# Decoder block on one core: smaller operation pieces, new orders on four engines, and two feed-forward products in each other's PSUM bank

## What is computed

```python
x = _layernorm(x + attn(x))        # silu(x Wq), silu(x Wk), rotary, decayed causal linear attention,
                                   # chunks of 128 with a carried state, 16 heads of 16,
                                   # o * sigmoid(x Wg1 Wg2), rms-norm per head, times weight, @ Wo
x = _layernorm(x + experts(x))     # 4 experts picked by token id: (silu(x Wg.T) * (x Wu.T)) @ Wd, all three = ctx
x = _layernorm(x + ffn(x))         # conv over two steps along the batch axis, silu; q, k, v, g products; rotary;
                                   # routed masked attention over 4 steps; norm per head; silu(g) * o @ Wout
```

## Time and profile before

| | us |
|---|---|
| median of 3 runs | 273.94 (273.74 to 274.32) |
| the profiled execution, its own time | 274.79 |
| its span, first to last instruction | 272.4 |
| PE busy | 188.1 (69%) |
| DVE busy | 158.8 (58%) |
| POOL busy | 104.3 (38%) |
| ACT busy | 88.2 (32%) |
| mean granted clock of PE | 0.876 of full |

### The profile page before, as it was taken

How to read it: one execution, slowest core, us unless ns; L and a number is a source line. 1 busy time by engine, 2 the same in 40 slices (tenths; PEclk the granted TensorE clock), 3 DMA queues, 4 the chain that set the end, 5 groups by cost and what they waited for, 6 DMA issues and landing times.

```text
span 272.4 us, 3513 instructions
## 1 busy us (share of the span) xinstructions
PE 188.1 (69%) x1066; PEld 122.6 (45%) x1066; DVE 158.8 (58%) x437; ACT 88.2 (32%) x227; POOL 104.3 (38%) x190
## 2 busy tenths in 40 slices
PE   3689999996939795957985068978427057872442
PEld 2277755563516362716874036747214034431221
DVE  1127767979794979581672072062397353599831
ACT  0065444452612452323422023543301014651121
POOL 9740107343550423120443540210433822764533
PEclk9999999999977999799999559999955759998557
DMA  7993051000000000040244700101100200110011
GB/s 199 316 348 128 2 215 56 2 1 0 23 0 0 20 2 19 2 150 6 93 166 167 250 22 0 40 3 37 39 19 0 58 20 0 39 40 0 0 39 39
DMA packets 16273, 17.44 MB, mean 64 GB/s; under 512 B 2928, under 2 KB 13696, under 8 KB 16256
## 3 DMA queue, kind: packets, MB, share of 16 engines
q1 hardware_dynamic: 13328, 14.57, 16.1%
q0 software_dynamic: 768, 2.10, 2.4%
q10 hardware_dynamic: 2160, 0.56, 1.1%
HBM read 7.79 MB, written 5.77 MB: 50 GB/s over the span
## 4 chain that ended last, share of the span: by engine, by line
PE 38%; DVE 30%; issue 10%; DMA 8%; POOL 6%; ACT 4%; SPq 1%; ACTq 1%; POOLq 0%; DVEq 0%
PE bank L1190 16%; PE bank L1248 7%; PE bank L1395 4%; PE bank L1410 4%; DMA w_qk<-in_L_attn_Wk 3%; PE bank L1185 2%; DVE rcos L835 2%; DMA yg<-ys_d,pos 2%; DVE newton L826 2%; DVE newton L825 2%; DMA xs<-xs_d 2%; POOL rstd L361 2%; DVE stats L887 2%; PE bank L1292 2%; POOL yg L407 1%
## 5 line engine op out<-in xcount | busy, mean ns | idle before, releaser
L1248 PE MATMUL bank<-qx,kT 128*128 128x512 f32 x64 | 33.3, 646 | 13.3 <-DVE probs L857 12.0
L1190 PE MATMUL bank<-f_w,oT 128*128 128x512 f32 (+4 forms) x80 | 31.8, 549 | 5.8 <-ACT oT L643 5.8
L358 POOL TENSOR_SCALAR rstd<-agg 128x1 f32<-128x1 f32 x24 | 5.7, 239 | 70.7 <-DVE agg L889 70.3
L572 ACT ACTIVATE qx<-bank,con 32x256 f32<-32x256 f32 x64 | 26.3, 458 | 15.9 <-PE bank L1185 15.3
L1190 PEld LDWEIGHTS bank<-f_w,oT 128*128 128x128 f32 x80 | 16.2, 213 | 19.3 <-issue 8.9
L1248 PEld LDWEIGHTS bank<-qx,kT 128*128 128x128 f32 x64 | 11.8, 197 | 28.7 <-issue 26.4
L344 POOL TENSOR_TENSOR rsin<-qk,rope_tab 128x256 f32<-128x256 f32 x16 | 12.5, 802 | 31.8 <-ACT qk L555 31.7
L857 DVE TENSOR_TENSOR probs<-bank,con 128x512 f32<-128x512 f32 x32 | 21.5, 686 | 5.4 <-PE bank L1248 5.0
L958 DVE TENSOR_TENSOR rsin<-rcos,bank 128x512 f32<-128x512 f32 (+1 forms) x8 | 5.0, 620 | 27.3 <-ACT rcos L620 27.3
L1410 PE MATMUL bank<-slot_w,rsin 128*128 128x256 f32 x56 | 14.9, 409 | 8.2 <-DVE rsin L958 8.2
L1190 PE MATMUL bank<-w_qk,xT 128*128 128x512 f32 x32 | 17.2, 665 | 2.2 <-DMA w_qk<-in_L_attn_Wk 2.2
(11 more groups left out here) (149 smaller groups left out, 410.6 us busy)
## 6 DMA issues: line engine op xcount, KB each, us to landing
slot_w<-ctxT SPq DMA_DIRECT2D x14, 256.0 KB, 2.3
xs_d<-xs SPq DMA_DIRECT2D x2, 896.0 KB, 8.3
xs<-xs_d SPq DMA_DIRECT2D x2, 896.0 KB, 5.3
ys_d<-qkr SPq DMA_DIRECT2D x6, 256.0 KB, 2.2
x_sb<-in_x SPq DMA_DIRECT2D x4, 256.0 KB, 7.6
ctx_sb<-in_ctx SPq DMA_DIRECT2D x1, 1024.0 KB, 11.2
out<-x_sb SPq DMA_DIRECT2D x8, 128.0 KB, 1.7
con<-shape_constants SPq DMA_DIRECT2D x1, 402.5 KB, 3.1
```

What stands on the lines that cost most here:

```text
L358: eng.tensor_scalar(rstd[:, n, i:i + 1], agg[:, n, i, 1:2], LN_EPS, None, ALU.add)\
L572: eng.activation(qx[rr, i % 2, :, 2 * r + par, :], two(bank[2][rr, 0:2 * P]), ACT.Copy, scale=con[rr, C_PARITY + par:C_PARITY + par + 1]). ...
L1190: last = eng.matmul(dst, lhsT[:, k, :], w[:, k, :], start=(k == 0), stop=(k == KT - 1))
L1248: eng.matmul(bank[3 + g % 2][:, :], kT[:, i % 2, g // 2, :], qx[:, i % 2, g // 2, 4 * (g % 2):4 * (g % 2) + 4, :].rearrange("p h n -> p (h ...
```

## The change

The change does five things.

1. It cuts operations into smaller pieces: `proj_qkv` into `proj_qk`, `proj_v` and (with the first loop) `proj_gate`; `transpose_qk` into `turn_q` and `turn_k`; `attend(i)` into `attend(i, g)` for g = 0 to 3; `norm_o` into `square_o` and `root_o`; the turning of the experts' weights, the router weights and the centring of the value weights into calls of their own. Each piece keeps its instructions and takes the waits that it needs.
2. It drops `attention_round` from use. PE, DVE, ACT and POOL each get a new flat list of all calls from the first to the last. Nothing is computed that was not computed before, and the counts of operations are the same but for four more ACT_TABLE_LOAD on ACT (eight in place of four), since silu and sigmoid now alternate at the start.
3. `load_slots` issues four transfers, one per item, in place of one.
4. The q-v-k product of `project_step` goes to bank 4, and `project_out` to bank 6, with the waits that the banks' earlier users need.
5. The wait for cleared buffers at the head of ACT's list moves to the first `copy_v` and `expand_q`.

```diff
             def load_slots(c):
                 eng.wait_ge(S_(f"scattered{c}"), 16 * L)
-                if c:
-                    eng.wait_ge(S_("xsT_made"), len(ITEMS))
-                eng.dma_start(xs[:, :, :], xs_d[c][:, :].rearrange("(s q) d -> q s d", q=P)).then_inc(S_("xs_in"), 16)
+                for m, (s0, s1) in enumerate(ITEMS):
+                    if c:
+                        eng.wait_ge(S_("xsT_made"), m + 1)
+                    eng.dma_start(xs[:, s0:s1, :], xs_d[c][s0 * P:s1 * P, :].rearrange("(s q) d -> q s d", q=P))\
+                       .then_inc(S_(f"xs_in{c}{m}"), 16)
...
-            def attend(i):
+            def attend(i, g):
...
-                for g in range(4):
-                    eng.wait_ge(S_("probs"), 4 * i + g + 1)
+                eng.wait_ge(S_("probs"), 4 * i + g + 1)
...
-            def norm_o(i):
+            def square_o(i):
...
+                if i:
+                    eng.wait_ge(S_("o_rstd"), i)
                 eng.tensor_reduce(oms[:, :], heads(osq[:, i % 2, :]), AX.X, ALU.add).then_inc(S_("o_ms"), 1)
+
+            def root_o(i):
                 eng.wait_ge(S_("o_ms"), i + 1)
...
                 else:
                     eng.wait_ge(S_("wv_centred"), 2)
-                    eng.wait_ge(S_("ln0_sum"), TILES)
-                project(bank[6][:, :], uT[:, j % 2, :, :], f_w1[:, :, :]).then_inc(S_("f1_made"), 1)
+                    eng.wait_ge(S_("probs"), 4 * TILES)
+                project(bank[4][:, :], uT[:, j % 2, :, :], f_w1[:, :, :]).then_inc(S_("f1_made"), 1)
...
+                else:
+                    eng.wait_ge(S_("ln0_sum"), TILES)
                 for l in range(l0, l1):
-                    project(bank[4][:, (l - l0) * D:(l - l0 + 1) * D], fT[:, l - l0, :, :], f_out[:, :, :])\
+                    project(bank[6][:, (l - l0) * D:(l - l0 + 1) * D], fT[:, l - l0, :, :], f_out[:, :, :])\
...
             route_weights(0)
             weigh_values(0)
+            gate_values(0)
+            gather(4)
+            gather(5)
+            gather(6)
+            gather(7)
+            ln_rstd(1, 4)
+            scale_values(0)
...
-            for i in range(TILES - 1):
-                attention_round(i)
...
+            proj_qk(4)
+            turn_expert(2)
+            turn_expert(3)
+            turn_q(1)
+            turn_k(1)
+            scores(0, 0)
```

More of the change, by code:

```diff
@@ L1332, in attention_round @@
             def attention_round(i):
[L1333 removed]
+                turn_q(i)
+                turn_k(i)
                 if i == 0:
[L1335 removed]
+                    for n in range(E):
+                        turn_expert(n)
                     rank_tokens()
                 if 0 <= i - 1:
[L1338 removed]
+                    for g in range(4):
+                        attend(i - 1, g)
                 if i < L:
@@ L1479, in _ @@
-            transpose_qk(7)
-            attend(6)
-            for g in range(4):
-                scores(7, g)
+            turn_wg1()
+            transpose_x(0)
+            transpose_x(1)
+            make_wg()
+            proj_v(0)
+            transpose_x(2)
+            proj_gate(0)
+            proj_qk(0)
+            transpose_x(3)
+            transpose_x(4)
+            proj_gate(1)
+            proj_gate(2)
+            proj_gate(3)
+            transpose_x(5)
+            transpose_x(6)
@@ new lines, in _ @@
+            scores(2, 0)
+            scores(2, 1)
+            attend(1, 0)
+            attend(1, 1)
+            attend(1, 2)
+            attend(1, 3)
+            turn_k(3)
+            transpose_on(0)
+            proj_qk(5)
+            scores(2, 2)
+            scores(2, 3)
+            make_state(3)
+            scores(3, 0)
+            scores(3, 1)
+            project_o(0)
+            turn_back(1)
+            attend(2, 0)
+            attend(2, 1)
+            attend(2, 2)
+            scores(3, 2)
@@ new lines, in _ @@
+            proj_v(4)
+            attend(2, 3)
+            scores(3, 3)
+            turn_q(4)
+            turn_back(2)
+            proj_qk(6)
+            proj_v(5)
+            attend(3, 0)
+            attend(3, 1)
+            attend(3, 2)
+            attend(3, 3)
+            turn_q(5)
+            turn_k(4)
+            transpose_on(1)
+            proj_qk(7)
+            turn_k(5)
+            scores(4, 0)
+            scores(4, 1)
+            project_o(1)
+            scores(4, 2)
@@ new lines, in _ @@
+            attend(4, 0)
+            turn_back(3)
+            scores(4, 3)
+            attend(4, 1)
+            scores(5, 0)
+            turn_k(6)
+            turn_q(6)
+            attend(4, 2)
+            transpose_on(2)
+            attend(4, 3)
+            scores(5, 1)
+            proj_v(6)
+            turn_k(7)
+            scores(5, 2)
+            scores(5, 3)
+            project_o(2)
+            turn_q(7)
+            attend(5, 0)
+            turn_back(4)
+            attend(5, 1)
```

736 lines of the change are left out of this document (496 added, 240 removed).

## The result

| | us |
|---|---|
| median before (4 runs beside it) | 274.13 (273.74 to 275.01) |
| median after (4 runs) | 226.31 (224.66 to 228.00) |
| ratio, with its 95% interval | 0.825 (0.818 to 0.832) |
| the profiled execution after, its own time / its span | 224.66 / 222.6 |

In a later batch the same kernel had a median of 223.99 (223.48 to 229.74, 6 runs), so it spreads more than before did. Four of these six took 223.5 to 224.0 us and two 228.2 and 229.7.

A forecast was written before the change was run, and what follows sets the result against it. No engine was full; in attention DVE and PE were near full, DVE tighter, and later waits left half 1 nearly alone. Terms 116 + 27.5 + 8 + 26.5 + 9.5 + 53.5 gave 241.0 us of span, hence 242.5 us; range 231 to 258.

The forecast's parts named there:

- End of the masks: Start through attention's last mask: first mask at 41.3 us, masks ending at 116, 6.6 us sooner.
- DVE then has 64.7 us of work left: Masks' stretch: DVE's busy work from the first mask on, with 10.2 us of waits added.
- the narrower: Masks' stretch before: DVE (70.2 of 88.6 us busy) and PE (73.6) near full, DVE taken as the tighter limit.
- End of masks to first gather: Last mask to first gather of half 0: 27.5 us, 0.7 sooner; PE's item queue unchanged.
- Gather to h2: First gather of half 0 to first h2 transposition: unchanged at 8.0 us, PE's first half 1 item filling the gap.
- h2 to gathers of half 1: First h2 transposition to half 1's first gather: 26.5 us, 27.2 sooner, set by PE's work before the last down product.
- Gather to step 4: Half 1's first gather to tile 4's feed-forward product: 9.5 us, 0.5 later; bounds 9 to 13.
- Step 4 to the end: Last stretch: 53.5 us, 2.6 later; half 0's leftover DVE work mostly fits into waits, but the end chain stays unfilled.
- Banks: Exchange of banks for the feed-forward products: costs nothing; if not, half a microsecond.
- Table loads: Start, ACT: eight loads instead of four add 5.1 us, helping put the first mask at 41.3 us, not 34.
- better case: DVE waits only 5 us in attention and the last stretch takes 50: 234 us, chance 0.10.
- the rivals: No attention gain (249.5 us, 0.17); half 0 leftover unhidden (254.2, 0.13); better (234, 0.10); PE clock falls (0.04); no effect (0.01).

The follow-up runs named there:

- a1: Changed kernel's functions (four slot loads, exchanged banks, attend in four pieces) with every engine in the order of the kernel before: 270.31 us.
- b1: Changed kernel with one more score product on PE in each of tiles 1 to 7: 229.11 us.
- b2: Changed kernel with nine more mask products on DVE into an unread tile: executions of 224.93, 226.60, 230.61 and 231.08 us.
- a2: Changed kernel with the new lists up to the last masks and the old order behind them: 254.27 us.
- a3: Changed kernel with the old lists up to the last masks and the new order behind them: 243.47 us.
- c2: Changed kernel with one load of all slots of a half (896 KB) in place of four: 230.32 us.
- a4: As a1, but POOL's four half 1 gathers stand behind weigh_values(1), and DVE's residual2(4) and residual2(5) before head_var(1): 268.92 us.
- e1: Changed kernel with twelve more DVE reductions into an unread tile, four each ahead of the steps of groups 2, 3 and 4: 227.55 us.
- c1: Changed kernel with the feed-forward's q-v-k and output products back in banks 6 and 4, without the added waits: 225.96 us.
- c3: Changed kernel with ACT's eight sigmoids in one run and PE's gate products 5 to 7 earlier, for fewer table loads: 227.32 us.
- d0: Changed kernel unaltered, measured again in a later batch: 223.99 us.
- d2: d1 plus the edit of c3 (sigmoids in one run, gate products 5 to 7 earlier): 228.58 us.
- b3: Changed kernel with POOL turning the keys of steps back 2 and 3 inside attention instead of before the first mask: 230.03 us.
- c4: Changed kernel with tile 7's way to the slots moved earlier on PE and ACT, and half 1's slot loads before half 0's last store: 230.92 us.
- d1: Changed kernel with DVE's mark_experts moved from behind copy_xT(2) to behind copy_kT(0): 230.12 us.
- d3: d1 with SP's load of half 1's slots ahead of the fetch of slot 6's weights: 231.20 us.

## Why the forecast was wrong

**End of the masks** (116, measured 106.0): the step that failed is "DVE then has 64.7 us of work left", with a wait of 10.2 us laid on top. It had 55.8. The waits (10.6) came out as forecast by chance, since they are now DVE's waits for PE, and the first mask came 1.7 us sooner than forecast. Of the 8.9 us, some 5 are the root chains: 15.5 us for 60 steps in a1 (L912, L914 to L916) against 10.4 after. Cosines, squares and scalings, slowed in the same way, add 1.1 (by their means in the two kernels). The other 2.6 are work put in the wrong place: a third cosine, one scaling of h and one difference of the router weights no longer stand in the stretch (0.9, 0.5, 0.4), and the square and the sum of tile 6 do not come into it (0.8). I took durations of DVE from a trace in which POOL stood beside them, as if they were fixed, and moved POOL's work away without pricing it.

The second fault weighs more: I called DVE "the narrower" and made the sum for DVE alone. PE's sum is 73.6 us less three q-k products (24 matmuls stand there in a1 and 12 after, 6.0 us) and one v product (1.0) = 66.6 us, which from 39.6 on ends at 106.2. The longer of the two sums sets the end, and that is PE's, as b1 and b2 show; b2 also shows that 4.7 us of work put back on DVE cost 2.0, so right durations alone would not have mended the forecast much. That 66.6, worked out with the result at hand, comes so near the measured 66.26 is in part luck: it leaves out the first item of the experts, whose turning and upward products came into the stretch (2.6 us), and what PE's score and output products gained as the clock went from 0.94 to 1.00 (1.6 us, 32.5 to 31.5 and 5.8 to 5.2).

**End of masks to first gather** (27.5, measured 23.7): what failed is "PE is busy 21.5 of it and the queue of items is the same". PE is busy for 18.50 us: the first item's 20 matmuls (2.6 us) were done before the last mask. a2, with the new attention and the old lists behind it, has 22.2 us here, and a3, with the old attention and the new lists behind, 26.9, so the gain is the new attention's. On the old order the four loads shorten the stretch by 2.4 us (25.8 in a1), but in the new order by less than 1 (24.5 in c2).

**Gather to h2** (8.0, measured 8.5): right. The first item's product fills the gap as said, though PE stood idle 5.96 us ahead of it, and the split of the load is what keeps the 8.5 (10.3 in c2).

**h2 to gathers of half 1** (26.5, measured 24.8): the mechanism was right, PE's work in front of the last down product, which ends 21.4 us behind the transposition (20 and one wait of 1.8 were priced). The further 1.8 us for waits between engines was too much. a4 shows that the view from which I started, POOL's gathers behind a scaling, named the wait but not the gain.

**Gather to step 4** (9.5, measured 11.7): within its bounds; a4, where DVE also has more to do here, has 14.7.

**Step 4 to the end** (53.5, measured 47.9): DVE's work was put at 39.9 and is 38.25, and its density at 0.79 and is 0.80. What failed is the allowance for a chain "that nothing fills", 3 us on top of 50.5: e1 speaks for DVE's work as the bound instead.

**Banks** (nothing): right, c1. **Table loads**: the first mask's forecast (41.3, measured 39.6) came out near, by luck: c3 shows that it was not the loads, of which there were six more and not four. PE, almost without idle time from 6.8 us on, is busy for 32.4 us ahead of the first mask where it was 26.0, which covers the 5.6 us by which the mask came later.

The six terms missed by -10.0, -3.8, +0.5, -1.7, +2.2 and -5.6 us, 18.4 in all. Half of it is the one term of attention. The range ended at 231 since its better case changed the waits alone and never the work. Of the rivals none occurred: PE's clock rose to 1.00 in attention instead of falling.

## What to carry to other kernels

Where a change reorders everything, make the sum of work for each engine and let the longest set the stretch; waits shown before do not carry over. A duration of DVE taken from beside a busy POOL is not its own duration: compare repetitions of the same step, and price what moving the neighbour does. Then put wide POOL products where DVE waits anyway and where nothing that PE needs stands behind them on POOL, and take loads apart where the first consumer needs only a piece.

## What the runs showed of the hardware

- A chain step of 128x16 on DVE takes 0.17 us alone and up to 0.65 beside a POOL product; steps of 128x8 go from 0.20 (0.59 for three) to 0.6 us (1.82 for three). The masks, which read PSUM, keep their time (682 to 686 ns).
- The last stretch comes in lengths that go with PE's granted clock, with DVE's work the same (38.0 to 38.3 us): 45.9 to 46.1 us at 0.85 to 0.89 (b1, c1, d0, d2), 47.6 to 47.9 at 0.79 to 0.83 (after, a3, b2, b3, c2), 48.2 to 48.4 at 0.75 (c3, c4, d1, d3). Which of the two is the cause wasn't tried.
- A store of 128 KB took 3.0 us from issue to the gather that waits for it; behind four loads on the same queue it took 4.9 (c4).
- A load of 896 KB was there 5.4 us after its issue (c2), the first of four loads of 256 KB issued together after 3.3.
- After a wait of 2.3 to 3.0 us behind the marks PE's granted clock was 0.50, 0.61 and 0.58 from 18 to 22 us (b2, c2, c4), where it was 1.00 from 10 to 30 us in the profiles without that wait.
